# A rotation's cosine product moved from GpSimd to VectorE, and two regroupings of TensorE's queue

## What is computed

```python
# L0 attention: 16 heads of 32 channels, window of 64 keys
q, k, v = split(layernorm(x) @ w_qkv.T)
q = q * cos + rotate_half(q) * sin          # the rotation ("rope"), the same for k
k = k * cos + rotate_half(k) * sin
scores = where(keep, q k^T * scale, -inf)
x = x + softmax(scores) v @ w_out.T
# L0 cross attention to ctx_2048
q = layernorm(x) @ Wq.T + bq; k = ctx @ Wk.T + bk; v = ctx @ Wv.T + bv
x = x + layernorm(rs * (softmax(clip(q k^T)) v @ Wo.T + bo)) * gamma + beta
...
```

## Time and profile before

| | |
|---|---|
| three runs | 3090.97, 3095.11, 3095.7 us; median 3095.11 |
| the profiled execution | 3092.49 us, of which the span of the profile is 3090.8 |
| TensorE busy | 2936.7 us, 95% of the span, mean granted clock 0.983 |
| VectorE, ScalarE, GpSimd busy | 2313.8, 1599.6, 779.2 us (75, 52, 25%) |
| phase 1 | about the first 730 us of the span |

### The profile page before, as it was taken

One profiled execution on the slowest core, in us unless ns is written; L12 is line 12 of the kernel. 1 busy time (PEld: TensorE's weight loads), 2 busy tenths in 40 slices (PEclk: granted clock), 3 DMA queues, 4 the chain that ended last, 5 costly groups with the idle time before them and its releaser, 6 DMA issues. The chain is left out here.

```text
span 3090.8 us, 61869 instructions
## 1 busy us (share of the span) xinstructions
PE 2936.7 (95%) x23041; PEld 2393.6 (77%) x23041; DVE 2313.8 (75%) x4355; ACT 1599.6 (52%) x3677; POOL 779.2 (25%) x940
## 2 busy tenths in 40 slices
PE   7999999998999999999999879999999989999999
PEld 5677677775998888888888756767676678888888
DVE  4666666665876788888888678878786887777776
ACT  3334433444222555555555447676666765555555
POOL 1221122122664111111111173433422022222222
PEclk9999999999999999999999989999999999999999
DMA  7233343332311777777777632222210132222222
GB/s 283 89 120 120 134 140 113 127 127 78 119 56 56 248 253 242 254 244 250 244 250 248 244 111 73 59 69 59 66 42 18 42 121 78 80 76 76 76 69 72
DMA packets 146029, 403.97 MB, mean 131 GB/s; under 512 B 38976, under 2 KB 47680, under 8 KB 133008
## 3 DMA queue, kind: packets, MB, share of 16 engines
q1 hardware_dynamic: 107888, 325.36, 30.6%
q0 software_dynamic: 18464, 50.45, 5.5%
q10 hardware_dynamic: 19456, 25.18, 2.3%
HBM read 344.06 MB, written 54.76 MB: 129 GB/s over the span
## 5 line engine op out<-in xcount | busy, mean ns | idle before, releaser
L3147 POOL TENSOR_TENSOR mixf<-act 128x256 f32<-128x256 f32 x128 | 143.3, 1119 | 458.3 <-DVE act L3413 458.3
L292 POOL DMA_INDIRECT hr<-normed_rows,idx x96 | 95.6, 995 | 643.1 <-PE psum L316 588.8
L341 PE MATMUL psum<-xT_hi,wgu_hi 128*128 128x192 f32 (+1 forms) x1536 | 227.9, 270 | 1.8 <-DVE xT_lo L328 1.0
L173 POOL TENSOR_SCALAR ve<-mv 128x1 f32<-128x1 f32 x112 | 35.9, 321 | 756.2 <-DVE mv L1076 493.7
L341 PE MATMUL psum<-xT_hi,wgu_lo 128*128 128x192 f32 (+1 forms) x1536 | 223.1, 267 | 0.0
L341 PE MATMUL psum<-xT_lo,wgu_hi 128*128 128x192 f32 (+1 forms) x1536 | 222.7, 267 | 0.0
L1871 ACT ACTIVATE eth<-psum 128x192 f32<-128x192 f32 (+1 forms) x192 | 63.3, 330 | 299.1 <-PE psum L341 292.5
L341 PEld LDWEIGHTS psum<-xT_hi,wgu_hi 128*128 128x128 f32 (+1 forms) x1536 | 189.8, 182 | 27.1 <-ACT wgu_hi L1855 21.5
L2441 ACT ACTIVATE scratch<-psum,smin 128x512 f32<-128x512 f32 x256 | 174.0, 687 | 62.1 <-DVE smin L2887 60.4
L341 PEld LDWEIGHTS psum<-xT_lo,wgu_hi 128*128 128x128 f32 (+1 forms) x1536 | 190.3, 182 | 0.0
L341 PEld LDWEIGHTS psum<-xT_hi,wgu_lo 128*128 128x128 f32 (+1 forms) x1536 | 190.2, 182 | 0.0
(11 more groups left out here) (484 smaller groups left out, 8695.2 us busy)
## 6 DMA issues: line engine op xcount, KB each, us to landing
w_sg<-in_w_gu_dram SPq DMA_DIRECT2D x32, 1408.0 KB, 6.1
w_su<-in_w_gu_dram SPq DMA_DIRECT2D x32, 1408.0 KB, 6.4
w_slot<-w_split SPq DMA_DIRECT2D x21, 2048.0 KB, 8.4
w_raw<-in_w_dram SPq DMA_DIRECT2D x128, 256.0 KB, 2.6
w_sd<-in_w_d_dram SPq DMA_DIRECT2D x32, 512.0 KB, 8.5
wd<-in_w_d_dram SPq DMA_DIRECT2D x32, 512.0 KB, 8.2
expert_out<-so ACTq DMA_DIRECT2D x64, 256.0 KB, 5.2
w_slot<-w_split SPq DMA_DIRECT2D x28, 512.0 KB, 4.3
```

The costliest lines, as they stand in the source:

```text
L292: pool.indirect_dma_start(out=xg[:, t, :], out_offset=None, in_=rows, in_offset=bass.IndirectOffsetOnAxis(ap=idx[:, t:t + 1], axis=0)).the ...
L341: ins = pe.matmul(bank(2 + m)[0:w, gu * CAP:(gu + 1) * CAP], wgu2[wp][:, gu, kc, m0:m0 + w], xT2[xp][:, kc, :], start=(i == 0 and kc == 0) ...
L3147: pool.tensor_tensor(mixf[:, g % LAG, :], act2[:, g % LAG, 0, :], act2[:, g % LAG, 1, :], ALU.add).then_inc(sy["f_mix"], 1)
```

## The change

Three edits, all in `phase1`:

1. GpSimd's loop of cosine products is gone; its two root computations for the output norm (`rstd_pool(norm_out)`) now directly follow those for the delta. In `rope` VectorE makes the cosine product itself, between the sine product and the sum.
2. In turns 1 to 7 `values(i, 0)` stands directly behind `queries_keys(i)` on TensorE, ahead of the first scores, and ScalarE's copy of that tile ahead of its exponentials.
3. In all turns the last but one chunk of `cross_values(1)` stands behind the first turned tile, and the last chunk behind the second.

```diff
@@ GpSimd
-                for n in range(KC):
-                    pool.wait_ge(sy["qk_raw_ready"], due("qk_raw_ready", i, 2 * n + 2))
-                    if n >= 2:
-                        pool.wait_ge(sy["rope_ready"], due("rope_ready", i, n - 1))
-                    m = ROPES[n]
-                    pool.tensor_tensor(cosq2[n % 2][:], qk_raw[:, 2 * m:2 * m + 2, :],
-                                       cosT[:].unsqueeze(1).broadcast_to([P, 2, S]), ALU.mult
-                                       ).then_inc(sy["rope_cos_ready"], 1)
-                    if n == 1 and i >= 1:
-                        rstd_pool(pool, sy, norm_out(i - 1), mv, ve, rstd, const["minus_half"])
+                    rstd_pool(pool, sy, norm_out(i - 1), mv, ve, rstd, const["minus_half"])
@@ ScalarE
+                if i >= 1:
+                    values_copy(i, 0)
                 for n in range(LPAIRS):
...
-                    if n < NT:
+                    if n < NT and (i == 0 or n >= 1):
                         values_copy(i, n)
@@ TensorE
                 queries_keys(i)
+                if i >= 1:
+                    values(i, 0)
                 for n in range(LPAIRS + 4):
                     if n < LPAIRS:
                         scores(i, n)
                     if n == 1:
-                        for j in range(NT):
+                        for j in range(0 if i == 0 else 1, NT):
                             values(i, j)
...
                 cross_values(0, 2, KC)
-                cross_values(1, 0, KC - 1)
+                cross_values(1, 0, KC - 2)
                 turn_tile(h, normed_attn(i), turned_attn(i), 0)
+                cross_values(1, KC - 2, KC - 1)
+                turn_tile(h, normed_attn(i), turned_attn(i), 1)
                 cross_values(1, KC - 1, KC)
-                turn_tile(h, normed_attn(i), turned_attn(i), 1)
@@ VectorE, rope
                 ln(dve.tensor_tensor(sinq[:], sinq[:], sinT[:].unsqueeze(1).broadcast_to([P, 2, S]), ALU.mult))
-                dve.wait_ge(sy["rope_cos_ready"], due("rope_cos_ready", i, n + 1))
+                ln(dve.tensor_tensor(cosq2[n % 2][:], qk_raw[:, 2 * m:2 * m + 2, :],
+                                     cosT[:].unsqueeze(1).broadcast_to([P, 2, S]), ALU.mult))
                 dve.tensor_tensor(qk[:, 2 * m:2 * m + 2, :], cosq2[n % 2][:], sinq[:], ALU.add
```

## The result

The change makes the kernel slower: 3110.9 us (3106.3 to 3115.2) against 3094.1 us before (3091.0 to 3095.7), a ratio of 1.0051 with a 95% interval of 1.004 to 1.0063. I had said 3087, with a range of 3078 to 3099; the sign was wrong, and the time lies outside the range.

A forecast was written before the change was run, and what follows sets the result against it. TensorE's waits in phase 1 were taken as the bound, with 24 us of rotation wait and low clock at the first edit. Terms summed to -7.9 us: 3092.5 profiled to 3084.6, said as 3087 for the median, range 3078 to 3099.

The forecast's parts named there:

- Start of the first value tile: Turns 1 to 7, TensorE: the wait for a rotation becomes a wait for the value weights' transfer; +2.4 us.
- The clock at that place: First value tile, turns 1 to 7: low clock costing 12.1 us mostly returns, less falls worth 4 us; -8 us.
- Rotations: VectorE takes GpSimd's product; the chain behind the first scores runs level with TensorE, 0.2 us a turn; +1.4 us.
- Cross values: All eight turns: a chunk fills the wait for the turned tile's copy, 0.7 us a turn; -5.6 us.
- Turn 0: Value order kept, but weight splits queue behind VectorE's rotations and TensorE's value tiles wait for the last; +1.2 us.
- Shifted values: Shift on SP issued some 1.5 us later, just behind the row store, against its reader `local_values`; +0.7 us.
- rival D: VectorE, with all four products of a rotation, and the shift behind it become the bound; 3093.5 us, chance 0.11.

The follow-up runs named there:

- `no_rot`: The changed kernel with GpSimd's product with the cosines kept, value tiles and cross values as changed; 3094.5 us, 0.9997 of the kernel before.
- `shift_first`: The changed kernel with the shifted values' two transfers issued on SP ahead of the row store; 3087.7 us, 0.9981 of the kernel before.
- `shift_copy_first`: `shift_first` with ScalarE also copying the second value tile ahead of the second pair's exponentials; 3092.0 us, 0.9991 of the kernel before.
- `half_ahead`: The changed kernel with only the row store's first half (512 KB) ahead of the shift, the other half behind; 3091.7 us, 0.9992 of the kernel before.
- `cross_only`: The kernel before with only the cross values edit, rotations and value tiles as before; 3090.6 us, 0.9983 of the kernel before.
- `shift_act`: The changed kernel with ScalarE issuing the shift on its own queue, SP loading cross-query weights once it landed; 3139.6 us, 1.015 of the kernel before.
- `no_order`: The changed kernel with both value tiles back behind the second pair of scores; 3086.7 us, 0.9974 of the kernel before.
- `store_held`: The kernel before with the row store held until the second value tile is copied, right ahead of the shift; 3111.2 us, ratio 1.0062.

## Why the prediction was wrong, step by step

- **Start of the first value tile**, +2.4 forecast: 14.9 - 11.9 = +3.0. Right, with the cause named.
- **The clock at that place**, -8 forecast: right, at its good end, and that end was luck. From the mask product or value tile to `local_values`, without the wait for the shift, seven turns took 105.0 us before and 95.0 after (13.6 each). Seven times turn 2's 13.27 (229.98 to 243.25) is 92.9, so the clock's 12.1 came back in full; that they were the clock's stands on the stretches of turns 2 and 3 in the earlier trace rows. But with the tile at the same place the clock fell there in one turn of seven in `no_rot`, in two in `shift_first` and `shift_copy_first` and in three in `half_ahead`, at some 1.5 us a fall; the two falls that I had reckoned with are the middle of these five profiles. The fall of turn 3 before began among the score products (0.50 from 318.2 to 325.0), 2 us ahead of the stretch of the earlier trace rows.
- **Rotations**, +1.4 forecast: the remaining 95.0 - 92.9 = +2.1 holds more than them. `no_rot`, without their edit, takes 13.42 a turn where the clock holds, so they make 0.15 a turn, about +1.0, and the other +1.0 comes with the new place of the tile. Right, with a small term for the place left out.
- **Cross values**, -5.6 forecast: 4 to 5 us in `cross_only`, near it. **Turn 0**, +1.2: the turn is 0.3 us longer with its gain of 0.7 from the cross values in it, so about +1.0 (an estimate). Near it.
- **Shifted values**, +0.7 forecast: +10.4. This step failed. I saw the shift come later against its reader and the store just ahead of it, and still bounded it by its landing time alone, 2.4 us, at 0.8 a turn at most. It lands in 3.8 us beside the store, and the wait is 1.15 to 1.24 us a turn and once 3.28 (a shift that took 5.7 us; why is open).
- **The clock behind it**, no term in my sum: from `local_values` to the output projection the seven turns took 85.9 us before and 99.6 after, +13.7. In turns 1, 4 and 6 that stretch took 17.7, 16.2 and 16.4 us instead of 12.36.

Together: 3.0 - 12.1 + 2.1 - 4.8 (cross, turns 1 to 7) + 0.3 (turn 0) + 10.4 + 13.7 = +12.6 of the 13.7; about 1 us lies elsewhere. Without the last two terms it is -11.5; `shift_first`, which removes them, was 10.6 us below before in its profile, and 6 us (0.9981) over all runs, near the forecast of 3087 with 3087.7. So the sign that I had given for rival D came true, `local_values` waiting for the shift by over half a microsecond; I had given D 0.11 and 0.9 us a turn, without a price for the clock. D's reason was half of it: VectorE's products lengthened the wait, but 4.9 of its 10.4 us are there without them (`no_rot`). The delay beside a store is real (3.8 us for 2.4), but a place behind the store in SP's queue is not needed for it, since ScalarE's queue gave the same 3.8 us.

Before, the clock's falls cost up to 2.97 us a turn at the scores, and I took that as the price of a fall. Behind `local_values` a fall cost 3.9 to 5.4. So the two steps that failed are the bound on the shift's wait, which took a time to landing measured alone for one beside a store, and the missing price for what the clock does after such a wait.

## What to carry to other kernels

The time to landing of a lone transfer is no bound once other transfers are under way (2.4 and 3.8 us here): look at what is issued in the microsecond ahead of it on any queue (in turn 3 the store stood 0.75 us ahead on the same queue after the change, 0.70 us ahead on another in `shift_act`), and put the small transfer that someone waits for ahead of the large one that nobody does. When an edit delays an instruction, ask of every list behind it what now stands close together: here a store that waits for VectorE and a shift that waits for ScalarE met on SP. And a new wait of TensorE can cost more than its length (10.4 us of waits came with 13.7 us more in the work behind them here); give it a price for the stretch that follows it, not the price of falls seen elsewhere.

## What was not expected of the hardware

- A shift of two transfers of 128 KB took 2.4 us alone and 3.8 beside 1 MB of stores, on SP's queue and on ScalarE's alike, and 2.4 with 512 KB ahead. I had held it possible that on a queue of its own it lands in 2.3 to 2.7 us although the store is under way (the first theory of `shift_act`); here it did not.
- The length of a low clock went with the place of the fall. Falls at the value tile or the scores before it lasted 3.4 to 6.8 us in the records; those with waits of `local_values` or of the scores beside it 10 to 17 us. What ends them is not shown.
- Of 11 waits for the shift between 1.15 and 1.63 us (after, `no_rot`, `no_order`, `store_held`) 5 came with a fall (a record of the clock at 0.50 that begins in the wait or at most 2.2 us behind it); one of 1.22 did and another did not, so the wait's length alone does not tell. None up to 1.05 us did; the one of 3.28 did, and so did the wait for exponentials in all seven turns of `shift_act`.
- Waits of 1.6 to 2.75 us for the value weights, with wide products on both sides, came with a fall in none of seven turns after the change, one in `no_rot`, two in `shift_first` (some 1.55 us each) and three in `half_ahead`: the same wait goes either way.
